# Feed-forward of a gated block: x and z turned by transposing DMAs, two PSUM banks at a time, normalisation on ScalarE, weights laid out ahead

## The chip, the cores and the metric

One core of a Trainium2 chip runs the whole program. The metric is the device time of one execution in microseconds (us); the median of three runs stands for a kernel. A core has five engines that run side by side and meet only at semaphores: TensorE (PE in the rows), VectorE (DVE), ScalarE (ACT), GpSimd (POOL) and SyncE (SP), which here only issues DMAs. Each engine works through its own instructions in order; an instruction that waits holds up everything behind it on its engine.

## The reference

2048 tokens of width 512 (x is 4 x 512 x 512). First an expert layer: each token goes to one of four experts, chosen by its id; expert e has one 512 x 512 matrix, used three times (ctx_2048 is passed as gate, up and down weight). Then a feed-forward layer with quantised operands.

```
x = x + tanh(g_xattn) * experts(layernorm(x), token_ids, ctx, ctx, ctx)
x = x + tanh(g_ffn)   * ffn(layernorm(x), gate_w, gate_b, val_w, val_b, out_w, out_b)

experts: e = min(id // 6250, 3);  y = (silu(h @ W[e].T) * (h @ W[e].T)) @ W[e].T
bit_linear(x, w, b):                      # D = 512, H = 2048
    scale_x = 127 / max(abs(x), per token)
    xq = round(x * scale_x) / scale_x     # clipped to -128..127
    wq = clip(round(w / mean(abs(w))), -1, 1) * mean(abs(w))
    return xq @ wq.T + b
ffn(x) = bit_linear(silu(bit_linear(x, gate)) * bit_linear(x, val), out)
```

## The kernel before

**Routing.** The token ids are sorted by expert into 19 units (`UNITS`) of 128 rows, none with rows of two experts. POOL gathers the rows of a unit from memory by an indirect DMA (`gather`) and, when the unit is finished, scatters the rows with their mean, 1/deviation and token number to a buffer in memory, `x1_rows`, by another (`scatter`).

**Expert units.** Weights and activations are split into a high and a low float16 part, so that a product is 12 matmuls of 512 columns (`product`, line 494). ctx arrives with the wrong axis on the partitions, so TensorE turns it in 16 groups (`ctx_group`, 458); ScalarE makes `w_hi` from PSUM and VectorE `w_lo` (883), four of them POOL. `slot(j)` of TensorE (523) is: turn gu of unit j-1, the first product of unit j, turn h of unit j+1, the second product of unit j-1. VectorE's loop over j (976) makes the normalised rows (`norm`), the low parts (`h_low`, `gu_low`), the product gu, the new rows x1 and their statistics. POOL's loop (361) makes 1/deviation of unit j+2 (`unit_rstd`), that of the finished rows (`x1_rstd`), scatters unit j-2, gathers unit j+4, and rounds two pairs of weight groups (`round_pair`, 341) in twelve consecutive passes, from j = 7 (`W_SLOT` = 8). ScalarE sums their absolute values (`sum_abs`) in units 0 to 11 and takes the sign (`sign_pair`) after the rounding. The three weight matrices are 24 pairs of 128 x 512 groups (`PAIRS`); after the sign TensorE turns each pair in eight transposes (`turn_pair`, 513) and VectorE copies it back (`keep_pair`, 933).

**Hand-over.** SP waits until units 0 to 15 are scattered, then loads the first two tiles of the feed-forward stage (`EARLY`, 256); POOL scatters unit 16 only after these loads have landed (309 to 312). After unit 18 it loads the others.

**Feed-forward stage.** 16 tiles of 128 tokens. Per tile TensorE does 32 matmuls for gate and value (`gate_val`, 579: four chunks c of 512 columns, four matmuls each for gate and value), 16 for the output (`down`, 598), 4 transposes of the quantised x (`turn_x`) and 16 of the quantised z (`turn_z`). The work on a tile is spread over three slots: gate and value of tile t, the quantising of z of tile t-1, and the output of tile t-2. For each chunk VectorE scales PSUM and adds the bias (`pre_gate`, `pre_val`), ScalarE does silu, POOL multiplies the two (`z_chunk`, 385) and VectorE takes the largest absolute value (`z_max`, 1053). From the four maxima come the scales (`z_max_all`, `z_gamma`, `z_scales`); ScalarE rounds z by adding a large number in two halves (`z_round`, 763), POOL subtracts it again (`unshift_z`, 377), TensorE turns each half into PSUM, and ScalarE copies it to SBUF (`z_keep`, 778). x goes the same way: VectorE normalises (`tile_norm`, 1012), ScalarE rounds and subtracts, TensorE turns, ScalarE copies. POOL adds the output bias to the rows and stores by an indirect DMA.

The order on every engine is written out by hand in the functions `ffn_slot` (TensorE 610, ScalarE 782, VectorE 1112) and `slot` (POOL 405); the middle tiles run in a loop with registers.

## Time and profile before

| | |
|---|---|
| median of three runs | 369.0 us (368.78 to 369.78) |
| the profiled execution | 367.59 us, its span 365.5 us |
| mean granted TensorE clock | 0.984 of full speed |
| start until the first product | 0 to 24.1 us |
| expert units | 24.1 to about 164.9 us |
| feed-forward stage | 164.9 us to the end |
| TensorE busy | 90% of the span |
| VectorE, GpSimd, ScalarE busy | 81%, 71%, 63% |

The span runs from the first to the last instruction that the profile records; 2.1 us of the profiled execution lie around it. Busy shares are averages over three stages with different limits, so a term of the change has to be read in its own stage. In a row of the timeline the first number is the start and the second the length, both in us; the brackets tell how long the engine had stood idle and what ended that.

### The profile page before, as it was taken

To read this page: it belongs to the slowest core of one execution; us is meant where nothing else is said; L and a number is where in the kernel's file an instruction comes from. 1 tells how busy PE (TensorE), PEld (TensorE's weight loads), DVE (VectorE), ACT (ScalarE), POOL (GpSimd) and SP (SyncE) were. 2 spreads that over 40 slices of the span, in tenths; PEclk is the share of its full clock that TensorE was granted. 3 is DMA by queue.
4 is the path that set the end of the run, shared out by engine and by line. 5 is a ranking of instruction groups with operands and counts; after the bars stand their busy time and mean duration, and the time that the engine had idled before them with its cause. 6 is when DMAs were issued, how large, how long until landed. Compare 5 with 4: busy or idle time off the path is not lost.

```text
span 365.5 us, 7169 instructions
## 1 busy us (share of the span) xinstructions
PE 328.6 (90%) x1976; PEld 177.8 (49%) x1992; DVE 294.5 (81%) x644; ACT 229.5 (63%) x327; POOL 259.4 (71%) x306
## 2 busy tenths in 40 slices
PE   2858899989998999789779999999999999999972
PEld 2734455546565555454335455544555455554440
DVE  5874777767787866788999899998999889998760
ACT  2837474657874456474467776687766877668650
POOL 2470366568878887847887888888888888888711
PEclk9979999999999999999999999999999999999997
DMA  6969257569312227231101101111011110110011
GB/s 244 302 225 388 57 208 266 179 203 248 126 58 65 84 84 275 70 89 34 32 2 29 59 31 58 58 30 58 29 58 55 31 58 29 59 47 11 29 39 49
DMA packets 24598, 37.03 MB, mean 101 GB/s; under 512 B 4543, under 2 KB 12735, under 8 KB 24320
## 3 DMA queue, kind: packets, MB, share of 16 engines
q1 hardware_dynamic: 20256, 23.38, 20.4%
q0 software_dynamic: 4320, 13.40, 10.6%
q8 instruction: 9, 0.15, 0.2%
q14 instruction: 13, 0.11, 0.1%
HBM read 28.35 MB, written 9.20 MB: 103 GB/s over the span
## 4 chain that ended last, share of the span: by engine, by line
PE 51%; POOL 17%; issue 10%; DVE 10%; DMA 6%; ACT 4%; POOLq 1%; SPq 0%; ACTq 0%; DVEq 0%
PE bank L587 25%; PE bank L605 15%; POOL raw L349 6%; PE bank L503 4%; PE bank L595 4%; POOL x_sb L331 3%; ACT tern L705 2%; POOL xg L302 2%; DMA x_rows<-x_sb,scatter_at 2%; POOL rstd L331 2%; DMA raw<-in_ctx 2%; POOL x_rows L315 1%; PE bank L469 1%; POOL var_eps L328 1%; POOL raw L388 1%
## 5 line engine op out<-in xcount | busy, mean ns | idle before, releaser
L587 PE MATMUL bank<-tern,raw 128*128 128x512 bf16 x512 | 118.2, 379 | 1.0 <-DVE raw L1042 0.7
L388 POOL TENSOR_TENSOR raw<-raw 128x512 f32<-128x512 f32 x63 | 80.3, 1278 | 21.5 <-ACT raw L776 18.1
L503 PE MATMUL bank<-w_hi,turned 128*128 x304 | 73.8, 386 | 9.1 <-DVE turned L915 7.9
L587 PEld LDWEIGHTS bank<-tern,raw 128*128 (+1 forms) x512 | 48.7, 98 | 55.3 <-ACT raw L761 1.3
L776 ACT ACTIVATE raw<-raw 128x512 f32<-128x512 f32 x64 | 39.9, 624 | 47.8 <-DVE raw L1042 46.3
L605 PE MATMUL bank<-tern,raw 128*128 128x512 bf16 x241 | 57.1, 379 | 3.7 <-ACT raw L780 1.9
L1042 DVE SCALAR_TENSOR_TENSOR raw<-bank,raw 128x512 f32<-128x512 f32 x64 | 47.6, 744 | 6.1 <-PE bank L587 5.4
L1050 DVE SCALAR_TENSOR_TENSOR raw<-bank,raw 128x512 f32<-128x512 f32 x64 | 47.6, 744 | 3.0 <-POOL raw L388 0.9
L503 PEld LDWEIGHTS bank<-w_hi,turned 128*128 128x128 f16 x304 | 29.8, 98 | 38.9 <-issue 13.8
L768 ACT ACTIVATE raw<-raw,magic 128x1024 f32 (+1 forms) x32 | 39.2, 1235 | 6.7 <-DVE raw L1069 6.7
L713 ACT ACTIVATE sign_sb<-raw,magic 128x1024 bf16<-128x1024 f32 (+1 forms) x24 | 27.2, 1148 | 25.9 <-POOL raw L349 25.7
L1055 DVE TENSOR_REDUCE raw<-raw 128x1 f32<-128x512 f32 (+1 forms) x64 | 43.1, 674 | 0.0
L503 PE MATMUL bank<-w_lo,turned 128*128 x152 | 39.9, 385 | 0.0
L382 POOL TENSOR_SCALAR raw<-raw,magic,one 128x1024 bf16<-128x1024 f32 x29 | 36.9, 1272 | 3.8 <-ACT raw L768 3.6
L605 PEld LDWEIGHTS bank<-tern,raw 128*128 128x128 bf16 x256 | 24.2, 98 | 29.4 <-ACT raw L780 2.3
L315 POOL DMA_INDIRECT x_rows<-x_sb,scatter_at x19 | 20.5, 1078 | 19.1 <-POOL x_sb L339 15.4
L780 ACT ACTIVATE raw<-bank 128x1024 bf16<-128x1024 bf16 x31 | 31.1, 1006 | 1.0 <-PE bank L595 1.0
L302 POOL DMA_INDIRECT xg<-in_x,gather_at x19 | 18.9, 994 | 16.1 <-DVE gather_at L875 9.3
L349 POOL TENSOR_SCALAR raw<-raw,inv_gam,magic 128x1024 f32<-128x1024 f32 x24 | 28.4, 1191 | 0.6
L893 DVE TENSOR_SCALAR h_sb<-xg,mean_var,rstd 128x512 f32<-128x512 f32 x19 | 11.2, 589 | 20.9 <-POOL rstd L331 19.0
L401 POOL DMA_INDIRECT out<-raw x16 | 16.6, 1038 | 13.9 <-DVE raw L1078 11.6
L705 ACT ACTIVATE tern<-raw 128x1024 bf16<-128x1024 f32 x24 | 25.3, 1053 | 1.1
(115 smaller groups left out, 477.4 us busy)
## 6 DMA issues: line engine op xcount, KB each, us to landing
raw<-x_rows SPq DMA_DIRECT2D x16, 257.5 KB, 2.6
raw<-in_ctx SPq DMA_DIRECT2D x4, 1024.0 KB, 8.2
raw<-in_L_ffn_gate_w SPq DMA_DIRECT2D x4, 1024.0 KB, 9.8
raw<-in_L_ffn_val_w SPq DMA_DIRECT2D x4, 1024.0 KB, 5.1
raw<-in_L_ffn_out_w SPq DMA_DIRECT2D x16, 256.0 KB
raw<-in_L_ffn_gate_b SPq DMA_DIRECT2D x1, 1024.0 KB
raw<-in_L_ffn_val_b SPq DMA_DIRECT2D x1, 1024.0 KB
xg<-in_x,gather_at POOLq DMA_INDIRECT x19, 3.8
```

Of the source, the lines that this page charges most:

```text
L349: nc.gpsimd.tensor_scalar(w, w, inv_gam[:, m:m + 1], magic[:, 0:1], ALU.mult, ALU.add).then_inc(rounded, 1)
L382: nc.gpsimd.tensor_scalar(zi[:, a:b], zq[:, a:b], magic[:, 1:2], one[:, 0:1], ALU.add, ALU.mult).then_inc(zi_made[half], 1)
L388: nc.gpsimd.tensor_tensor(flat(z[:, bass.ds(t % 2, 1), c * D:(c + 1) * D]), s_post[:, c % 2, :], v_pre[:, c % 2, :], ALU.mult).then_inc(z_ ...
L503: last = nc.tensor.matmul(acc[:, :], a[:, k * P:(k + 1) * P], flat(w[:, bass.ds(e4 + k, 1), :]), start=(k == 0 and i == 0), stop=(k == KD ...
L587: last = nc.tensor.matmul(ps[c % 2][:, :].rearrange("p (a b) -> p a b", b=P), flat(xiT[:, bass.ds(t % 2, 1), k * P:(k + 1) * P]), rhs, sta ...
L605: last = nc.tensor.matmul(o_ps[:, :], ziT[:, k, :], tern[:, 2 * G + k, :], start=(k == 0), stop=(k == G - 1))
L705: nc.scalar.activation(flat(tern[:, 2 * p:2 * p + 2, :]), flat(raw[:, 2 * p:2 * p + 2, :]), ACT.Abs, accum_out=abs_sum[:, p:p + 1]).then_i ...
L768: nc.scalar.activation(zq[:, a:b], flat(z[:, bass.ds(t % 2, 1), a:b]), ACT.Identity, scale=flat(sc[:, bass.ds(t, 1), 12:13]), bias=magic[: ...
L776: nc.scalar.activation(s_post[:, c % 2, :], g_pre[:, c % 2, :], ACT.Silu).then_inc(s_made, 1)
L1042: v.scalar_tensor_tensor(g_pre[:, c % 2, :], g_ps[c % 2][:, :], col(t, 3), bias_g[:, c * D:(c + 1) * D], ALU.mult, ALU.add).then_inc(g_mad ...
L1050: v.scalar_tensor_tensor(v_pre[:, c % 2, :], v_ps[c % 2][:, :], col(t, 4), bias_v[:, c * D:(c + 1) * D], ALU.mult, ALU.add).then_inc(v_mad ...
L1055: v.tensor_reduce(col(t, 5 + c), flat(z[:, bass.ds(t % 2, 1), c * D:(c + 1) * D]), AX.X, ALU.max, apply_absolute_value=True).then_inc(zmax ...
```

## The change

**Layout of the weights.** The host now hands over ctx and the three weight matrices with the contracted axis on the partitions, 128 rows of contiguous data each. `ctx_group`, `turn_pair` and `keep_pair` are gone. `w_hi` and `w_lo` are made from SBUF in 8 pairs of 1024 columns instead of 16 groups of 512, all low parts by VectorE. `sign_pair` writes the finished pair. Rounding starts two units earlier (`W_SLOT` = 6). Three tiles are loaded early instead of two, each with its token column.

**Feed-forward stage.** z and x are turned by `dma_start_transpose` from SBUF to SBUF, issued by SP: two of 128 x 1024 for z and one of 128 x 512 for x per tile. `z_keep` and `x_keep` are gone. Gate and value are worked on in two pairs of 1024 columns, each two PSUM banks, instead of four chunks. Gate has two pairs of banks, value one. The second half of `unshift_z` moves from POOL to ScalarE. `tile_norm` moves from VectorE to ScalarE, as a multiplication by 1/deviation and an addition of a shift that VectorE makes (`tile_shift`), two tiles ahead. All loops but TensorE's are written out.

```diff
@@ POOL
+            def z_pair(t, c, width=2 * D):
+                pool.wait_ge(s_made, 2 * t + c + 1)
+                pool.wait_ge(v_made, 2 * t + c + 1)
+                nc.gpsimd.tensor_tensor(z[:, t % 2, 2 * D * c:2 * D * c + width], g_sb[:, c, 0:width],
+                                        v_sb[:, c, 0:width], ALU.mult).then_inc(z_made, 1)
...
+            for t in range(TILES):
+                if t >= 1:
+                    z_pair(t - 1, 1)
+                if t >= 3:
+                    store(t - 3)
+                if 1 <= t < TILES - 1:
+                    add_bias(t + 1)
+                if t >= 1:
+                    unshift_z(t - 1)
+                z_pair(t, 0)
@@ VectorE
+                    for p in range(6, E * KD // 2):
+                        w_low(p)
...
+            for t in range(TILES):
+                if t + 2 < TILES:
+                    tile_shift(t + 2)
+                pre_gate(t, 0)
+                if t >= 1:
+                    z_max(t - 1, 1)
+                    z_max_both(t - 1)
                     z_gamma(t - 1)
                     z_scales(t - 1)
+                pre_val(t, 0)
+                if t + 2 < TILES:
+                    x_max(t + 2)
+                    x_gamma(t + 2)
+                pre_gate(t, 1)
+                if t + 2 < TILES:
+                    x_scales(t + 2)
                 z_max(t, 0)
+                pre_val(t, 1)
+                if 2 <= t < TILES - 1:
+                    finish(t - 2)
@@ ScalarE
+            def ffn_slot(t, before=True, start=False, after=True):
+                if after:
+                    tile_norm(t + 2)
+                silu_gate(t, 0)
+                if before:
+                    z_round(t - 1, 0, start)
+                    z_round(t - 1, 1, start)
+                    unshift_z(t - 1, start)
+                silu_gate(t, 1)
+                if after:
+                    x_round(t + 2)
+                    x_unshift(t + 2)
@@ TensorE
+                pe.wait_ge(x_turned, 16 * (t + 1))
+                gate(t, 0, start)
+                val(t, 0, start)
+                if downs:
+                    down(t - 2, 0, start_down)
+                gate(t, 1, start)
+                val(t, 1)
+                if downs:
+                    down(t - 2, 1)
@@ SP
+            def turn_z(t, half):
+                sp.wait_ge(zi_made[half], t + 1)
+                if t >= 1:
+                    sp.wait_ge(z_read[half], t)
+                sp.dma_start_transpose(ziT[:, half * G // 2:(half + 1) * G // 2, :],
+                                       zi[:, half * H // 2:(half + 1) * H // 2]).then_inc(z_turned[half], 16)
...
+            for t in range(TILES + 1):
+                if 3 <= t < TILES - 1:
+                    load_tokens(t + 1)
+                if t >= 1:
+                    turn_z(t - 1, 0)
+                    turn_z(t - 1, 1)
+                if t + 2 < TILES:
+                    turn_x(t + 2)
+                if t + XT < TILES:
+                    load_rows(t + XT)
```

On POOL in the feed-forward stage, one tile (tile 3) of the kernel before; L388 is `z_chunk`, L395 the output bias, L382 `unshift_z`, L401 the store:

```order
L388 TENSOR_TENSOR raw<-raw 128x512 [waits v_made,s_made]
L395 TENSOR_TENSOR raw<-raw 128x512 [waits xn_made]
L388 TENSOR_TENSOR raw<-raw 128x512 [waits v_made,s_made]
L388 TENSOR_TENSOR raw<-raw 128x512 [waits s_made,v_made,ziT_done1,ziT_done0]
L382 TENSOR_SCALAR raw<-raw,magic,one 128x1024 [waits zq_made0,consts32]
L388 TENSOR_TENSOR raw<-raw 128x512 [waits v_made,s_made]
L382 TENSOR_SCALAR raw<-raw,magic,one 128x1024 [waits zq_made1,consts32]
L401 DMA out<-raw 2048x512 [waits o_made,consts32]
```

The same place of the changed kernel, where L387 is `z_pair`, L400 the store, L394 the bias and L381 `unshift_z`:

```order
L387 TENSOR_TENSOR w_both<-raw 128x1024 [waits v_made,s_made] x2
L400 DMA out<-raw 2048x512 [waits o_made]
L394 TENSOR_TENSOR raw<-raw 128x512 [waits xn_made]
L381 TENSOR_SCALAR w_both<-w_both,magic,one 128x1024 [waits z_turned0,zq_made0]
L387 TENSOR_TENSOR w_both<-raw 128x1024 [waits v_made,s_made] x2
```

Before, `unshift_z` of the former tile stood behind three of this tile's four multiplications; now it stands ahead of both.

On VectorE in the feed-forward stage of the changed kernel, from `pre_gate(t, 0)` (L922) on; L935 is `z_max`, L941 to L950 the scales of z, L930 `pre_val`, L902 to L912 the scales of x:

```order
L922 SCALAR_TENSOR_TENSOR raw<-banks,raw 128x1024 [waits z_made,g_done,xs2_made]
L935 TENSOR_REDUCE raw<-w_both 128x1 [waits z_made]
L941 TENSOR_SCALAR raw<-raw 128x1 [waits zmax_made]
L945 TENSOR_SCALAR raw<-raw 128x1 [waits z_step]
L949 RECIPROCAL raw<-raw 128x1 [waits z_step]
L950 TENSOR_TENSOR raw<-raw,out_gam 128x1
L930 SCALAR_TENSOR_TENSOR raw<-banks,raw 128x1024 [waits z_made,v_done]
L902 TENSOR_REDUCE raw<-raw 128x1 [waits xn_made]
L906 TENSOR_SCALAR raw<-raw 128x1 [waits x_step]
L922 SCALAR_TENSOR_TENSOR raw<-banks,raw 128x1024 [waits z_made,g_done]
L910 RECIPROCAL raw<-raw 128x1 [waits x_step]
```

Before, the same engine took these steps in chunks of 512, with four maxima per tile. Now `pre_val(t, 0)` stands behind the scales of the former tile, and three rows further on, after the two other scales of x, comes the maximum of the pair whose value part it made.

On VectorE at the start of the changed kernel, around unit 0 (L775 is `w_low`, L796 `h_low(1)`, L805 `gu_low(0)`):

```order
L796 SCALAR_TENSOR_TENSOR turned<-banks,turned 128x512 [waits hThi_made]
L783 TENSOR_SCALAR h_sb<-xg,mean_var,rstd 128x512 [waits rstd_made]
L835 TENSOR_TENSOR sign_sb<-sign_sb,banks 128x4
L837 TENSOR_SCALAR sign_sb<-sign_sb 128x19 [waits route_step]
L837 TENSOR_SCALAR sign_sb<-sign_sb 128x19 x2
L838 TENSOR_SCALAR sign_sb<-banks 128x19
L839 TENSOR_TENSOR sign_sb<-sign_sb 128x19 [waits route_step]
L775 SCALAR_TENSOR_TENSOR w_both<-raw,w_both 128x1024 [waits whi_made,route_step]
L775 SCALAR_TENSOR_TENSOR w_both<-raw,w_both 128x1024 [waits whi_made]
```

The two L775 rows are new here; `gu_low(0)` comes behind them.

## Rows read from the trace of the kernel before

**Rows 1.** The page: busy times of the engines, and the chain's shares by engine

```profile
PE 328.6 (90%) x1976; PEld 177.8 (49%) x1992; DVE 294.5 (81%) x644; ACT 229.5 (63%) x327; POOL 259.4 (71%) x306
...
PE 51%; POOL 17%; issue 10%; DVE 10%; DMA 6%; ACT 4%; POOLq 1%; SPq 0%; ACTq 0%; DVEq 0%
```

**Rows 2.** One steady tile: length, then busy PE, PEld, DVE, ACT, POOL, clock

```profile
212.86:224.34 11.48, 11.43 (x68) 5.79 (x69) 10.52 (x24) 8.39 (x11) 9.70 (x9) 1.00 0.16 47
```

**Rows 3.** That tile by line: count, busy us, mean ns of one, idle before

```profile
L587 PE MATMUL bank<-tern,raw 128*128 128x512 bf16 x32 | 7.4, 379 | 0.0
L388 POOL TENSOR_TENSOR raw<-raw 128x512 f32<-128x512 f32 x4 | 5.1, 1279 | 1.3 <-ACT raw L776 1.2
L605 PE MATMUL bank<-tern,raw 128*128 128x512 bf16 x16 | 3.9, 379 | 0.1
L1042 DVE SCALAR_TENSOR_TENSOR raw<-bank,raw 128x512 f32<-128x512 f32 x5 | 3.7, 742 | 0.1
...
L1055 DVE TENSOR_REDUCE raw<-raw 128x512 f32 x4 | 2.7, 674 | 0.0
L382 POOL TENSOR_SCALAR raw<-raw,magic,one 128x1024 bf16<-128x1024 f32 x2 | 2.6, 1282 | 0.3 <-ACT raw L768 0.3
...
L768 ACT ACTIVATE raw<-raw,magic 128x1024 f32 x2 | 2.5, 1236 | 0.3 <-DVE raw L1069 0.3
...
L595 PE MATMUL bank<-ident,raw 128*128 128x128 bf16 x16 | 1.2, 219 | 0.0
...
L576 PE MATMUL bank<-ident,raw 128*128 128x128 bf16 x4 | 0.4, 219 | 0.0
```

**Rows 4.** Timeline of the hand-over: x1 behind the bias loads, scatter, first loads, first gate

```profile
147.44 0.75 DVE L921 SCALAR_TENSOR_TENSOR x_sb<-bank,y_scale,xg 128x512 f32<-128x512 f32 x1 [2.71 <-DMA x_rows<-x_sb,scatter_at]
...
151.48 1.07 POOL L315 DMA_INDIRECT x_rows<-x_sb,scatter_at  x1 [0.81 <-POOL x_sb L339]
...
154.64 0.33 SPq L249 DMA_DIRECT2D raw<-x_rows  x1
...
164.87 5.35 PE L587 MATMUL bank<-tern,raw 128*128 128x512 bf16 x24 [0.22 <-ACT raw L761]
```

**Rows 5.** Timeline of POOL: gather of unit 9, first rounding, second

```profile
67.33 0.98 POOL L302 DMA_INDIRECT xg<-in_x,gather_at  x1 [0.30 <-issue]
...
81.44 2.37 POOL L349 TENSOR_SCALAR raw<-raw,inv_gam,magic 128x1024 f32<-128x1024 f32 x2
...
89.05 2.38 POOL L349 TENSOR_SCALAR raw<-raw,inv_gam,magic 128x1024 f32<-128x1024 f32 x2
```

**Rows 6.** All lines by form: POOL's two-input operation on one column

```profile
L328 POOL TENSOR_TENSOR var_eps<-mean_var,halves 128x1 f32<-128x1 f32 x19 | 3.5, 184 | 19.6 <-DVE mean_var L902 19.5
```

**Rows 7.** Timeline of the end: scales of the last z, its rounding, the last `finish`

```profile
348.81 0.69 DVE L1055 TENSOR_REDUCE raw<-raw 128x1 f32<-128x512 f32 x1
...
349.91 0.17 DVE L1069 RECIPROCAL raw<-raw 128x1 f32<-128x1 f32 x1
...
350.11 2.37 ACT L768 ACTIVATE raw<-raw,magic 128x1024 f32<-128x1024 f32 x2 [2.21 <-DVE raw L1069]
...
358.28 0.75 DVE L1078 SCALAR_TENSOR_TENSOR raw<-bank,raw 128x512 f32<-128x512 f32 x1 [4.41 <-PE bank L605]
```

**Rows 8.** Issues by line: KB of one, median us from issue to landing

```profile
raw<-x_rows SPq DMA_DIRECT2D x16, 257.5 KB, 2.6
...
raw<-in_L_ffn_gate_w SPq DMA_DIRECT2D x4, 1024.0 KB, 9.8
```

**Rows 9.** Timeline of VectorE: `norm` of units 0 and 1, `gu_low(0)`; TensorE: first product

```profile
19.67 1.38 DVE L893 TENSOR_SCALAR h_sb<-xg,mean_var,rstd 128x512 f32<-128x512 f32 x1 [1.97 <-issue]
...
26.53 0.55 DVE L893 TENSOR_SCALAR h_sb<-xg,mean_var,rstd 128x512 f32<-128x512 f32 x1 [1.10 <-POOL rstd L331]
...
33.38 0.69 DVE L915 SCALAR_TENSOR_TENSOR turned<-bank,turned 128x512 f16<-128x512 f32 x1 [0.49 <-ACT turned L696]
...
24.14 3.59 PE L503 MATMUL bank<-w_hi,turned 128*128 x8 [0.78 <-ACT w_hi L679]
```

**Rows 10.** Timeline of VectorE: the reciprocal of tile 0's z

```profile
183.40 0.15 DVE L1069 RECIPROCAL raw<-raw 128x1 f32<-128x1 f32 x1
```

719 lines of the change are left out of this document (250 added, 469 removed).

## The prediction

> **What bounds the kernel now.** I read the page first. TensorE is busy for 90% of the span and makes half of the chain that ended last; GpSimd makes another 17% of it [rows 1]. These are averages, so I cut the time into three stages. The last of them, the feed-forward stage, repeats one tile of 11.48 us, in which TensorE is busy for 11.43 us and all other engines less [rows 2]. There TensorE sets the pace. By line [rows 3], such a tile has 48 matmuls of 512 columns and 20 transposes. 24 such matmuls in a row take 5.35 us, of which the last one's latency is some 0.16, so one is 0.216 us [rows 4] and 48 are 10.4 us. The transposes are the other 1.1 us, and they are what the change takes off TensorE. In the expert units with rounding GpSimd sets the pace: its roundings follow each other every 7.61 us [rows 5]. The start is bound by a chain of small steps.
>
> **The feed-forward tile after the change.** With 48 matmuls TensorE needs 10.4 us. The question is whether another engine, or a circle of waits, needs more. Added up, no engine does: GpSimd has two multiplications of 1024, one rounding step, a bias and a store, 8.4 us; VectorE some 9.5, ScalarE some 8. But the orders of the four engines close a circle. From the scales of tile t-1: ScalarE rounds its first half; GpSimd subtracts (`unshift_z`), which now stands ahead of both multiplications of tile t; GpSimd multiplies pair 0; VectorE takes its maximum, and only then does `pre_val(t, 1)`; GpSimd multiplies pair 1; VectorE takes that maximum and makes the scales of tile t. Each step waits for the one before, by data or by its engine's order, so the sum is a period that no slack elsewhere shortens. Its terms:
> - ScalarE rounding, 1024 columns: 1.24, and GpSimd subtracting: 1.28 [rows 3].
> - Twice the multiplication of 1024. The trace has 512 columns at 1.279 [rows 3] and one column at 0.184 [rows 6], so a column costs 2.14 ns and 1024 cost 2.38. Doubling the instruction gives the upper bound, 2.56. Twice 2.38 is 4.76.
> - Twice the maximum: 0.674 for 512 [rows 3]; with 0.17 for one column [rows 7] as the fixed part that is 1.18, and doubled 1.35. Twice 1.18 is 2.36.
> - `pre_val`: 0.742 for 512 [rows 3], by the same way 1.31, doubled 1.48.
> - The three small steps from the end of the last maximum until ScalarE starts: 350.11 - 349.50 = 0.61 [rows 7].
> - Four other changes of engine. GpSimd stood idle 0.3 us ahead of two roundings [rows 3], 0.15 each; I take 0.1, so 0.4.
>
> The sum is 1.24 + 1.28 + 4.76 + 2.36 + 1.31 + 0.61 + 0.4 = 11.96 us. With the shorter GpSimd rounding of [rows 5] (2.37 / 2 = 1.19) and hops and overlaps cut to the least it is 11.5; with all doubled it is 13.0. I take 11.96, since both ends of the multiplication's line are in the trace. So taking 1.1 us off TensorE buys nothing here: 0.5 us per tile is lost.
>
> The Trainium skill, page GPSIMD Engine Reference, section 3.1, gives 4497 ns for a two-input operation of 2048 float32. By that 1024 would take 2.25 us and the circle 11.7, a forecast 4 us lower. No run here shows that width yet.
>
> **The transposes themselves.** Half of z is 256 KB from SBUF to SBUF. The trace has no such transfer. The nearest row in size is the load of 257.5 KB, which lands 2.6 us after its issue, and the longest landing of this queue is 9.8 us for 1 MB [rows 8]. I take 3. On SP `turn_z` waits for the reads of the tile before, and behind it stand `turn_x`, the row loads and the token loads; GpSimd's `unshift_z` waits for the transfer of a whole tile earlier. With 3 us each has 4 us or more to spare, so the price in a steady tile is nothing. The cover goes when two and a half such transfers fill the period: 11.96 / 2.5 = 4.8 us each. ScalarE's copies from PSUM (1.0 and 0.6 us) leave, a rounding step and `tile_norm` come; it has no part in the circle but `z_round`.
>
> **Start.** GpSimd no longer makes low parts during `norm(0)`, which falls from 1.38 to the 0.55 that `norm(1)` takes [rows 9], and no ctx groups stand between h and the first product. The product starts 1.9 us earlier than 24.14 [rows 9]. But VectorE makes two low parts of 1024 (1.2 each) ahead of `gu_low(0)` at 33.38 [rows 9]. That takes 2.4 us back for the second product. Some is caught up in unit 1, where TensorE had waited: net -0.8, between -2 and +1.
>
> **Expert units.** TensorE loses 192 transposes and VectorE 24 copies of 0.7, all in passes that GpSimd's 7.61 us bound; that is worth nothing. The rounding moves two passes forward. It could first stand at 67.33 + 1.03 = 68.4; two periods of 7.61 later is 83.6, where now it is 81.44 [rows 5]: +2.1. At the other end nothing comes back, since the scatter that SP waits for stands ahead of the last rounding now. The bias loads, which made VectorE wait 2.7 us [rows 4] where GpSimd did not yet need the result, fall two passes earlier, into a pass where it does: +1.0, between 0 and 1.9. SP's first load, at 154.64 [rows 4], comes at 154.6 - 0.8 + 2.1 + 1.0 = 156.9; call it L.
>
> **Hand-over.** The third tile with its tokens puts two more DMAs (0.45 each) ahead of the scatter of unit 16. Then GpSimd scatters 16, 17 and 18 until L + 14.0, adds two biases (2.2), multiplies (2.4), and through maximum, `pre_val`, second multiplication, maximum and scales (0.1 + 1.2 + 1.2 + 0.1 + 2.4 + 0.1 + 1.2 + 0.6) the first scales of z stand at L + 25.5. Before it was 183.55 - 154.64 = 28.9 [rows 4, 10]: 3.4 gained. The first gate product hangs on SP's transpose of x and starts some 10 us after L as before (164.87); it has 1.5 us of slack to the multiplication.
>
> **End.** 15 periods of 11.96, less 1.0 since GpSimd multiplies only 512 columns of the last pair. Before, the last scales stand at 350.08, `finish` starts 8.2 later and the span ends 7.2 after that [rows 7]. Now: VectorE is free 2.3 after the scales, subtracts twice (0.7), the second transpose lands 4.3 later behind the first, 8 matmuls (1.7): 9.3, and 7.2. That is 16.5; each microsecond of a transfer adds one.
>
> **The sum.** 156.9 + 25.5 + 179.4 - 1.0 + 16.5 = 377.3 us of span. The profiled execution has 2.1 more than its span and lies 1.4 under the median: 380.8 us.
>
> **The rivals.**
> - *TensorE's pace holds.* If a multiplication of 1024 cost 1.7 instead of 2.4, or the waits overlapped more than rows show, the period is 10.4 and the time 380.8 - 15 x 1.56 = 357.4. For it: every engine's own sum is under 10.4. Against: the price per column lies between two rows, and the circle is in the order itself. The point where it turns faster is a period of 11.2. With half-way periods 355 to 366. Chance 0.20.
> - *The transposes bound.* Over 4.8 us each they, and not the circle, set the tile. At 5.5 a tile is 13.8 and the time 408; at the 9.8 of the longest landing [rows 8] 24.5 and 569. For it: nothing in the trace shows such a transfer. Against: the same bytes as plain rows land in 2.6. Chance 0.10. The Trainium skill, VectorE: DVE Perf Modes, section The three transpose paths, gives 1309 ns for one square of 128 by DMA; eight in a row would be 10.5 us and the tile 26 us. No run here shows it.
> - *No difference.* The circle at its least (11.5: -6.9) and neither the earlier rounding (-2.1) nor the bias loads (-1.0) felt: 370.8, with a shorter transfer at the end 369. Chance 0.07.
> - *The forecast*, 370 to 390: 0.63.
>
> **How the numbers follow.** I forecast the likeliest, 380.8. The range 364 to 394 takes in the bounds of the period but its doubled end, the no-change case, and the near edges of the two others; about 2 in 10 stay out. A measurement here can tell about 0.3% (1 us) from no change. Faster by more has 0.20, within it 0.06, slower 0.74.
>
> **What would show it.** Right: a steady tile of 11.5 to 12.5 us with TensorE busy about 10.4 of it; the chain of waits going round GpSimd's multiplication, VectorE and ScalarE; 1024 columns on GpSimd at 2.3 to 2.5. Roundings every 7.6 us from about 68. TensorE waiting for VectorE's read of PSUM or for nothing at all, tile by tile, would decide between circle and rival one. A tile bound by SP, or z's transfers over 4.8 us, would show the second. I am wrong at the root if GpSimd's multiplication takes under 1.8.

## The result: 29 us slower, more than twice the forecast loss

| | before | after |
|---|---|---|
| median | 368.89 us (367.34 to 369.78) | 397.75 us (395.18 to 398.16) |
| ratio | | 1.077, 95% interval 1.071 to 1.083 |
| profiled execution, its span | 367.59, 365.5 us | 398.16, 396.4 us |
| steady feed-forward tile | 11.48 us | 12.81 us |

The prediction was 380.8 us, range 364 to 394. The sign was right, and so was the circle of waits through the engines, but the loss is 29 us where 12 were forecast, and the time lies above the range.

The page of the changed kernel, busy times and the chain's shares by engine, as in [rows 1]:

```profile
PE 304.7 (77%) x1399; PEld 141.7 (36%) x1416; DVE 284.0 (72%) x518; ACT 216.2 (55%) x267; POOL 235.6 (59%) x257
...
DVE 29%; PE 28%; POOL 24%; issue 12%; DMA 4%; ACT 1%; POOLq 1%; SPq 0%; DVEq 0%; ACTq 0%
```

TensorE has fallen from 90% to 77%. It made half of the chain before; now VectorE, TensorE and GpSimd share it. That is the picture of a circle through several engines. A steady tile, the columns as in [rows 2]:

```profile
249.90:262.70 12.80, 10.64 (x48) 4.53 (x48) 11.28 (x17) 7.76 (x8) 8.20 (x5) 1.00 0.42 94
```

TensorE is busy for 10.6 us of it, as the 48 matmuls ask, and waits for 2.2. The steps of the forecast circle, in the page's groups (busy time, mean ns of one, idle time before):

```profile
L387 POOL TENSOR_TENSOR w_both<-raw 128x1024 f32<-128x1024 f32 (+1 forms) x32 | 74.8, 2339 | 41.4 <-DVE raw L930 41.4
...
L935 DVE TENSOR_REDUCE raw<-w_both 128x1 f32<-128x1024 f32 x32 | 38.8, 1214 | 28.2 <-POOL w_both L387 28.2
L675 ACT ACTIVATE w_both<-w_both,magic,raw 128x1024 f32<-128x1024 f32 x32 | 38.0, 1233 | 21.6 <-DVE raw L949 21.6
...
L930 DVE SCALAR_TENSOR_TENSOR raw<-banks,raw 128x1024 f32<-128x1024 f32 x32 | 40.8, 1276 | 0.4 <-PE banks L524 0.4
...
L381 POOL TENSOR_SCALAR w_both<-w_both,magic,one 128x1024 bf16<-128x1024 f32 x15 | 17.9, 1193 | 28.4 <-ACT w_both L675 28.4
```

Each duration is within 0.1 us of its term: multiplication 2.34 (forecast 2.38), maximum 1.21 (1.18), rounding 1.23 (1.24), `pre_val` 1.28 (1.31), subtraction 1.19 (1.28). The idle times name the circle: GpSimd's multiplications waited 41.4 us for `pre_val` (L930), VectorE's maxima 28.2 us for the multiplications. And yet a tile is 12.81 us, not 11.96. What is in it that the sum has not? The timeline of VectorE and GpSimd through such a tile (L930 `pre_val(t, 1)`, L960 `finish`, L896 `tile_shift` of the tile after next, L922 `pre_gate(t+1, 0)`, L935 `z_max(t, 1)`, L949 the scales; L387 on POOL the multiplication of pair 1):

```profile
256.13 1.27 DVE L930 SCALAR_TENSOR_TENSOR raw<-banks,raw 128x1024 f32<-128x1024 f32 x1
257.32 0.74 DVE L960 SCALAR_TENSOR_TENSOR raw<-banks,raw 128x512 f32<-128x512 f32 x1
...
257.55 2.35 POOL L387 TENSOR_TENSOR w_both<-raw 128x1024 f32<-128x1024 f32 x1 [2.59 <-DVE raw L930]
...
257.98 1.93 DVE L896 SCALAR_TENSOR_TENSOR raw<-raw 128x1 f32<-128x1 f32 x1
259.84 1.27 DVE L922 SCALAR_TENSOR_TENSOR raw<-banks,raw 128x1024 f32<-128x1024 f32 x1
261.03 1.20 DVE L935 TENSOR_REDUCE raw<-w_both 128x1 f32<-128x1024 f32 x1
...
262.71 0.16 DVE L949 RECIPROCAL raw<-raw 128x1 f32<-128x1 f32 x1
```

`tile_shift` multiplies one column. It takes 1.93 us here and ends at 259.91, just as the multiplication does at 259.90. Behind it stands `pre_gate`, and only then the maximum, which could have started at 260.0 and starts at 261.03. In the first tiles the same instruction took 0.13 to 0.16 us; from 206.73 on it takes 1.93 or 1.94 in each of eleven tiles. It comes to stand beside the multiplication where `finish`, which the first two slots don't have, runs ahead of it. The changed kernel holds a first witness itself: from scales to scales it takes 12.80 to 12.82 us eleven times, once for each of these eleven rows, and 11.73 or 11.74 in three other periods. This is the theory that the experiments test: **an operation with two tensor inputs in SBUF stands still while GpSimd works on SBUF, and holds all that is behind it.** The rivals are that it waits for the loaded rows, or that the pace is set by something else, such as the transposes or the clock.

### The profile page after: what moved, and what is told of

Read it like the earlier page. It is cut to its first block, busy times and chain, and to the rows that moved or that the text cites. A ratio compares the mean times of both kernels' runs of the same rounds, so it can differ in the third digit from the quotient of the medians.

```text
span 396.4 us, 5102 instructions
## 1 busy us (share of the span) xinstructions
PE 304.7 (77%) x1399; PEld 141.7 (36%) x1416; DVE 284.0 (72%) x518; ACT 216.2 (55%) x267; POOL 235.6 (59%) x257
## 3 DMA queue, kind: packets, MB, share of 16 engines
HBM read 28.35 MB, written 9.20 MB: 95 GB/s over the span
## 4 chain that ended last, share of the span: by engine, by line
DVE 29%; PE 28%; POOL 24%; issue 12%; DMA 4%; ACT 1%; POOLq 1%; SPq 0%; DVEq 0%; ACTq 0%
PE banks L524 8%; PE banks L536 8%; POOL raw L356 7%; DVE raw L930 7%; PE banks L514 6%; DVE raw L896 5%; PE banks L461 5%; POOL xg L309 4%; DVE raw L935 4%; DVE raw L922 3%; POOL w_both L387 3%; POOL x_sb L338 3%; DMA x_rows<-x_sb,scatter_at 2%; POOL rstd L338 2%; POOL x_rows L322 2%
## 5 line engine op out<-in xcount | busy, mean ns | idle before, releaser
L461 PE MATMUL banks<-w_both,turned 128*128 x456 | 109.6, 392 | 23.1 <-DVE turned L805 21.2
L387 POOL TENSOR_TENSOR w_both<-raw 128x1024 f32<-128x1024 f32 (+1 forms) x32 | 74.8, 2339 | 41.4 <-DVE raw L930 41.4
L524 PE MATMUL banks<-tern,raw 128*128 128x512 bf16 x243 | 62.9, 394 | 34.3 <-DVE raw L930 33.5
L461 PEld LDWEIGHTS banks<-w_both,turned 128*128 128x128 f16 x456 | 45.7, 100 | 74.3 <-issue 32.5
L536 PE MATMUL banks<-tern,w_both 128*128 128x512 bf16 x255 | 63.6, 396 | 8.0 <-DMA w_both<-w_both 7.9
L514 PE MATMUL banks<-tern,raw 128*128 128x512 bf16 x254 | 60.2, 379 | 0.1
L935 DVE TENSOR_REDUCE raw<-w_both 128x1 f32<-128x1024 f32 x32 | 38.8, 1214 | 28.2 <-POOL w_both L387 28.2
L675 ACT ACTIVATE w_both<-w_both,magic,raw 128x1024 f32<-128x1024 f32 x32 | 38.0, 1233 | 21.6 <-DVE raw L949 21.6
L524 PEld LDWEIGHTS banks<-tern,raw 128*128 (+1 forms) x256 | 23.3, 100 | 72.4 <-DVE raw L930 47.4
L687 ACT ACTIVATE raw<-raw 128x1024 f32<-128x1024 f32 x32 | 33.6, 1050 | 16.3 <-DVE raw L922 16.3
L922 DVE SCALAR_TENSOR_TENSOR raw<-banks,raw 128x1024 f32<-128x1024 f32 x32 | 40.9, 1278 | 0.7 <-PE banks L514 0.7
L930 DVE SCALAR_TENSOR_TENSOR raw<-banks,raw 128x1024 f32<-128x1024 f32 x32 | 40.8, 1276 | 0.4 <-PE banks L524 0.4
L514 PEld LDWEIGHTS banks<-tern,raw 128*128 (+1 forms) x256 | 25.1, 98 | 30.4 <-issue 0.5
L381 POOL TENSOR_SCALAR w_both<-w_both,magic,one 128x1024 bf16<-128x1024 f32 x15 | 17.9, 1193 | 28.4 <-ACT w_both L675 28.4
L783 DVE TENSOR_SCALAR h_sb<-xg,mean_var,rstd 128x512 f32<-128x512 f32 x19 | 10.4, 546 | 29.8 <-POOL rstd L338 29.8
L400 POOL DMA_INDIRECT out<-raw x16 | 16.8, 1049 | 18.1 <-DVE raw L960 15.9
```

What stands on the lines that cost most here:

```text
L387: nc.gpsimd.tensor_tensor(z[:, t % 2, 2 * D * c:2 * D * c + width], g_sb[:, c, 0:width], v_sb[:, c, 0:width], ALU.mult).then_inc(z_made, 1)
L461: last = nc.tensor.matmul(acc[:, :], a[:, k * P:(k + 1) * P], flat(w[:, bass.ds(e4 + k, 1), :]), start=(k == 0 and i == 0), stop=(k == KD ...
L514: last = nc.tensor.matmul(g_ps[c][:, b, :], flat(xiT[:, bass.ds(t % 2, 1), k, :]), tern[:, k * HC + 2 * c + b, :], start=(k == 0), stop=(k ...
L524: last = nc.tensor.matmul(v_ps[:, b, :], flat(xiT[:, bass.ds(t % 2, 1), k, :]), tern[:, G + k * HC + 2 * c + b, :], start=(k == 0), stop=( ...
L536: last = nc.tensor.matmul(o_ps, ziT[:, k, :], tern[:, 2 * G + k, :], start=(k == 0), stop=(k == G - 1))
L675: nc.scalar.activation(zq[:, a:b], flat(z[:, bass.ds(t % 2, 1), a:b]), ACT.Identity, scale=flat(sc[:, bass.ds(t, 1), 12:13]), bias=magic[: ...
```

## Where the rest went

The span is 19.1 us longer than forecast: the first scales of z come 4.7 later (start and expert units 1.8, hand-over 2.9), the 15 periods take 187.4 us and not 178.4 (9.0), the end 22.0 and not 16.5 (5.5). In the 9.0 the held `tile_shift` is 11.8, and the rest of the circle is 2.8 shorter than forecast. The time is over its forecast by 17.0 only, since the sum had added 3.5 us from the span to the median, and it was 1.4. Start and expert units, timelines of POOL, VectorE and TensorE (first gather, `norm(0)`, first product, first rounding), as in [rows 5, 9]:

```profile
12.16 3.25 POOL L309 DMA_INDIRECT xg<-in_x,gather_at  x1 [8.96 <-DVE gather_at L765]
...
21.62 0.55 DVE L783 TENSOR_SCALAR h_sb<-xg,mean_var,rstd 128x512 f32<-128x512 f32 x1 [1.74 <-POOL rstd L338]
...
24.85 5.30 PE L461 MATMUL banks<-w_both,turned 128*128 x12 [1.50 <-DVE turned L796]
...
69.96 2.37 POOL L356 TENSOR_SCALAR raw<-raw,inv_gam,magic 128x1024 f32<-128x1024 f32 x2
```

`norm(0)` is as short as forecast, 0.55, but it comes 2 us later than before, because the first gather took 3.25 us to issue where the next took 0.97. VectorE made two low parts (two inputs in SBUF, 2.34 us from 12.03) meanwhile. The first product takes 5.30 us. That is no loss of the change: the row of 3.59 us in [rows 9] holds only the eight matmuls on `w_hi`, and the four on `w_lo` follow it in the kernel before:

```profile
27.52 1.88 PE L503 MATMUL bank<-w_lo,turned 128*128 x4
```

From 24.14 to 29.40 that product took 5.26 us, at a granted clock of 0.50 from 24 to 28 us. The slow clock of the start was there before.

The hand-over, timelines of SP, TensorE, POOL and VectorE (first row load, product of unit 18, first multiplication, first scales), as in [rows 4, 10]:

```profile
158.71 0.33 SPq L237 DMA_DIRECT2D raw<-x_rows  x1
...
165.65 5.20 PE L461 MATMUL banks<-w_both,turned 128*128 x12 [6.31 <-DVE turned L805]
...
177.86 2.36 POOL L387 TENSOR_TENSOR w_both<-raw 128x1024 f32<-128x1024 f32 x1
...
186.90 0.16 DVE L949 RECIPROCAL raw<-raw 128x1 f32<-128x1 f32 x1
```

The last product of the expert stage follows 6.3 us in which TensorE was idle, and takes 5.20 us instead of the usual 2.76. The scatter of unit 18 and the first multiplication come behind it. From the multiplication on the hand-over goes as forecast (9.2 us to the scales, forecast 9.3), so all of its 2.9 us are lost ahead of it.

The end, VectorE and TensorE, as in [rows 7], and the windows around it (length, busy PE, PEld, DVE, ACT, POOL, granted clock, share and GB/s of the DMA engines):

```profile
374.26 0.16 DVE L949 RECIPROCAL raw<-raw 128x1 f32<-128x1 f32 x1
...
377.37 1.29 DVE L1019 TENSOR_SCALAR w_both<-w_both 128x1024 bf16<-128x1024 f32 x2
...
383.14 6.54 PE L536 MATMUL banks<-tern,w_both 128*128 128x512 bf16 x16 [6.48 <-DMA w_both<-w_both]
...
389.72 0.75 DVE L960 SCALAR_TENSOR_TENSOR raw<-banks,raw 128x512 f32<-128x512 f32 x1 [11.07 <-PE banks L536]
```

```profile
378.00:382.00 4.00, 0.00 (x0) 0.00 (x0) 0.65 (x2) 0.00 (x0) 0.88 (x1) 0.60 0.72 143
382.00:386.00 4.00, 2.86 (x7) 1.04 (x8) 0.00 (x0) 0.00 (x0) 0.00 (x0) 0.50 0.34 54
```

TensorE idles for 6.5 us; the granted clock falls to 0.50, which is the lower of its two levels, 1.2 GHz, and the last 16 matmuls take 6.54 us, where 16 took 3.66 one tile earlier.

## The experiments

All start from the changed kernel. Times are medians; the ratios are to the kernel before (368.4 to 368.9 us on the same chips).

### One tensor input instead of two

```diff
-                v.scalar_tensor_tensor(col(t, 7), of[:, MEAN:MEAN + 1], -1.0, of[:, RSTD:RSTD + 1],
-                                       ALU.mult, ALU.mult).then_inc(shift_made, 1)
+                v.tensor_scalar(col(t, 7), of[:, MEAN:MEAN + 1], of[:, RSTD:RSTD + 1], -1.0,
+                                ALU.mult, ALU.mult).then_inc(shift_made, 1)
```

> One edit to the changed kernel: tile_shift (line 896, one column) reads 1/deviation as a scalar operand instead of as a second tensor, in the same place. Theory A (an operation with two tensor inputs in SBUF stands still while GpSimd multiplies, and holds pre_gate and z_max of the next step): the row falls from 1.93 us to 0.2, z_max(t,1) follows the end of GpSimd's multiplication by 0.1 instead of 1.13, and the late period falls from 12.81 to about 11.8; the time from 397.7 to 384 to 386. Rival B (the row is long because it waits for the loaded rows, or for anything but its own operands): the row stays 1.9 and the time 397 to 398. Rival C (any VectorE operation on those columns stands still beside GpSimd): the same as B. Rival D (the row does get short, but the pace is set by something else, such as the transposing DMAs or the clock): row 0.2, period still 12.5 to 12.8, time over 394.

386.48 us (385.75 to 387.06), ratio 1.050 (1.046 to 1.054): 11.3 us gained by one operand. Timeline of POOL and VectorE through a tile:

```profile
242.16 2.36 POOL L387 TENSOR_TENSOR w_both<-raw 128x1024 f32<-128x1024 f32 x1 [2.59 <-DVE raw L930]
...
242.60 0.20 DVE L896 TENSOR_SCALAR raw<-raw 128x1 f32<-128x1 f32 x1
242.72 1.27 DVE L922 SCALAR_TENSOR_TENSOR raw<-banks,raw 128x1024 f32<-128x1024 f32 x1
244.56 1.22 DVE L935 TENSOR_REDUCE raw<-w_both 128x1 f32<-128x1024 f32 x1 [0.57 <-POOL w_both L387]
...
245.76 1.27 POOL L394 TENSOR_TENSOR raw<-raw 128x512 f32<-128x512 f32 x1
...
246.25 0.17 DVE L949 RECIPROCAL raw<-raw 128x1 f32<-128x1 f32 x1
246.33 0.73 DVE L950 TENSOR_TENSOR raw<-raw,out_gam 128x1 f32<-128x1 f32 x1
```

The row is 0.20, beside the same multiplication; the maximum waits for GpSimd and for nothing else; the scales follow each other every 11.74 us. Theory A holds for this instruction, and rivals B, C and D fall. VectorE's L922 ran beside the multiplication for 1.27 us, not slower than alone: it has one input in PSUM and one in SBUF. And a second witness has appeared in the last row. L950, one column, two inputs in SBUF, took 0.14 in 15 of the 16 tiles of the changed kernel. Here it meets GpSimd's bias addition (245.76 to 247.03), takes 0.73 and ends at 247.06.

The Trainium skill, page SBUF — State Buffer, section Who interferes with whom, says that a VectorE instruction with two SBUF inputs contends with a GpSimd instruction that reads SBUF, and that the loser is blocked until the other's end, not slowed. The trace of the changed kernel agrees: 1.93 us for one column, ending with the multiplication.

The number of tensor inputs is not the whole rule, though. `norm(0)` of the kernel before is a TENSOR_SCALAR like the row of e1, with one tensor and two scalar operands, on 512 columns. It took 1.38 us from 19.67, where `norm(1)` took 0.55 [rows 9], and this is what GpSimd did meanwhile:

```profile
19.62 3.56 POOL L359 TENSOR_TENSOR w_lo<-tern,w_hi 128x512 f16<-128x512 f32 x3
```

No run here takes apart why that one was long and the one-column form of e1 never is.

### The same instruction elsewhere

```diff
+            tile_shift(2)
             for t in range(TILES):
-                if t + 2 < TILES:
-                    tile_shift(t + 2)
                 pre_gate(t, 0)
...
                 pre_val(t, 0)
+                if t + 3 < TILES:
+                    tile_shift(t + 3)
```

> One edit to the changed kernel: tile_shift with its two tensor inputs unchanged, but one tile further ahead and behind pre_val(t,0), where GpSimd does not multiply (it subtracts or is idle). Theory A: 0.15 to 0.3 us beside an idle GpSimd, at most 1.2 if the subtraction holds it as well; period 11.8 to 12.2, time 384 to 391. Rival B or C (the row is slow wherever it stands): 1.9 us there too; it then stands in the circle itself, so the time stays at 397 or rises. Rival D: row short, time over 394.

388.32 us (386.41 to 389.92), ratio 1.056 (1.051 to 1.060), 9.4 us gained; period 11.74. The instruction now mostly meets GpSimd's subtraction:

```profile
249.84 1.19 POOL L381 TENSOR_SCALAR w_both<-w_both,magic,one 128x1024 bf16<-128x1024 f32 x1 [0.77 <-ACT w_both L675]
...
250.22 0.82 DVE L896 SCALAR_TENSOR_TENSOR raw<-raw 128x1 f32<-128x1 f32 x1
```

It is held there too, until 251.04 (the subtraction ends at 251.03), though that GpSimd operation has only one tensor input. But nothing of the circle waits for what stands behind it, and the period is that of e1. A stall costs what is queued behind it, not its own length. In slot 0 the moved instruction asks for the rows of tile 3 before they are there. It waits 3.81 us for their DMA with all of VectorE's work behind it, and the first scales stand at 189.58 instead of 187.54 in e1. That is the likely source of the 1.8 us between the two medians, though in the two profiled executions the end gives it back: both spans are 384.7.

### The circle cut

The edit of e1, and:

```diff
                 if t + 2 < TILES:
                     x_scales(t + 2)
+                pre_val(t, 1)
                 z_max(t, 0)
-                pre_val(t, 1)
```

> The edit of e1, and on VectorE pre_val(t,1) ahead of z_max(t,0) instead of behind it. My prediction's circle (period = ScalarE rounding + GpSimd subtraction + two multiplications with a maximum and pre_val between them + maximum + scales) loses 1.2 + 1.3 us by it, 9.3 us are left, and TensorE with 48 matmuls at 0.216 should set the pace: period 10.4 to 10.7, TensorE busy all of it, time 366 to 371. If the transposing DMAs are not hidden (the rival of the prediction): TensorE waits for them, period 11 or more, time over 374. If the circle is not what sets the pace: the time of e1, 384 to 386.

360.98 us (360.85 to 361.38), ratio 0.981 (0.977 to 0.984): 1.9% faster than the kernel before, and 36.8 us faster than the changed one, by one operand and two exchanged lines. The period is 10.36 us, with TensorE busy for all of it:

```profile
235.10:245.46 10.36, 10.36 (x50) 4.69 (x48) 9.72 (x17) 7.76 (x8) 8.20 (x5) 1.00 0.55 116
```

So the circle was the bound, with 1.2 + 1.3 us of it in that order of two lines, and without it TensorE's 48 matmuls are. Each transposing DMA is hidden.

> Only the reordering of e3; tile_shift keeps its two tensor inputs and its place. By theory A the maximum and finish (1.2 + 0.7 us) now lie between the start of GpSimd's multiplication of pair 1 and tile_shift, so it is held for 0.4 to 0.6 us only, behind which pre_gate still comes in time: period 10.4 to 10.9, time 367 to 374. If the stall costs the same wherever the order puts it: about 1 us per tile more than e3, 381 to 385.

The exchange of the two lines alone, with `tile_shift` as it was, gives 365.01 us (363.4 to 367.89), ratio 0.992 (0.989 to 0.995), a little under what I expected and 4.0 over e3. The steady period is 10.36 as well. VectorE's rows, and POOL's two multiplications and bias addition, which the first of them meets:

```profile
178.56 4.67 POOL L387 TENSOR_TENSOR w_both<-raw 128x1024 f32<-128x1024 f32 x2
183.19 1.08 POOL L394 TENSOR_TENSOR raw<-raw 128x512 f32<-128x512 f32 x1
...
182.09 2.21 DVE L896 SCALAR_TENSOR_TENSOR raw<-raw 128x1 f32<-128x1 f32 x1
...
194.41 1.47 DVE L896 SCALAR_TENSOR_TENSOR raw<-raw 128x1 f32<-128x1 f32 x1
...
246.66 0.67 DVE L896 SCALAR_TENSOR_TENSOR raw<-raw 128x1 f32<-128x1 f32 x1
```

0.67 us in the steady tiles is covered, as expected. In the first two slots `finish` is absent, and there it is held for 2.21 (until 184.30, past the multiplications and to the end of the bias addition at 184.27) and for 1.47 on the path: the first scales come at 187.09 instead of 184.99, the second at 198.67 instead of 194.22. The price of the same stall is 0 or some 2 us, by what stands behind it.

### What the transposes cost

On e3, behind each half of z in the queue of SP, in tiles 1 to 8:

```diff
+                if 1 <= t < 9:
+                    spare = raw_flat[:, 2 * G * D + (2 * t - 2 + half) * D:2 * G * D + (2 * t - 1 + half) * D].bitcast(bf16)
+                    sp.dma_start_transpose(spare.rearrange("p (h m) -> p h m", m=P),
+                                           flat(tern[:, 2 * half:2 * half + 2, :])).then_inc(spare_turned, 16)
```

> On e3, two more transposing DMAs of 128 x 1024 per tile in tiles 1 to 8, from the weights to free memory, behind each half of z in SP's queue; nothing reads them. They nearly double the traffic of the transposes. My prediction (not felt in a steady tile until two and a half transfers fill the period): with 1.2 us of issue and about 1.7 us of DMA time each, the queue is at some 85%; x and the second half land 1.3 to 3 us later, which the orders cover: period 10.36 in tiles 1 to 8 as in 9 to 14, time 361 to 362. Rival (the transposes are close to the bound): the period of the doubled tiles is 11 to 14, time 366 to 390.

361.19 us (360.45 to 361.26), ratio 0.979 (0.976 to 0.982), as e3. The scales follow each other at 10.36 with twice the transposes of z as without. The DMA view of 200 to 262 us, share of the queue, and then medians to landing:

```profile
q1 hardware_dynamic: 30649, 8.75, 74.4%
...
raw<-tern SPq DMA_TRANSPOSE x13, 3.2
w_both<-w_both SPq DMA_TRANSPOSE x12, 3.2
...
raw<-raw SPq DMA_TRANSPOSE x6, 3.8
```

The queue's share is 74.4% where e3 has 46.0%. Only x's transposes land later, 3.8 instead of 2.5 us. The second rival of the prediction is refuted with room to spare.

### The clock behind idle time

On e3, extra matmuls into a free bank (`keep_clock(n, acc)` issues n of 512 columns):

```diff
+            pe.wait_ge(whi_made, 1)
+            keep_clock(32, bank[4])
             turn_h(0)
...
+            keep_clock(27, bank[4])
             e4 = expert_of(UNITS - 1)
             pe.wait_ge(guTlo_made, UNITS)
...
             for t in range(TILES - 3, TILES):
+                if t == TILES - 1:
+                    for _ in range(26):
+                        nc.tensor.matmul(bank[3], tern[:, 0, 0:P], tern[:, 0, :], start=True, stop=True)
                 down(t, 0)
```

> On e3. Extra matmuls without a use, into a free bank, where TensorE stood idle longest: 32 ahead of turn_h(0), 27 ahead of the product of unit 18, 26 ahead of the last tile's down. Theory (the matmuls behind long idle time are slow because the granted clock has fallen to the half, 1.2 of 2.4 GHz): the 16 last matmuls fall from 6.28 to about 3.6 us, the 12 of unit 18 from 5.10 to about 2.8, the first product from 4.16 to about 2.8, the first transposes of h from 1.12 to 0.6. End -2.7, hand-over -2.3, start up to -1.9 as far as it is felt: 354 to 357. Rival (they are slow because their weights or data arrive late, or because GpSimd and the DMAs hold the path): their length stays, time 361 or later by what the extra matmuls delay. A second rival: the clock rises, but the stages wait for something else just behind (scatter, store), and under 2 us are gained.

357.17 us (356.09 to 358.38), ratio 0.969 (0.965 to 0.973), 3.8 less than e3. TensorE's timeline:

```profile
24.48 5.30 PE L465 MATMUL banks<-w_both,turned 128*128 x12 [1.50 <-DVE turned L806]
...
165.42 2.76 PE L465 MATMUL banks<-w_both,turned 128*128 x12 [0.89 <-DVE turned L815]
...
344.82 3.40 PE L542 MATMUL banks<-tern,w_both 128*128 128x512 bf16 x15 [0.94 <-DMA w_both<-w_both]
```

The product of unit 18 falls from 5.10 (e3) to 2.76, the last matmuls from 6.28 to some 3.6 (one of the 16 is missing in the record). These two were slow by the clock.

What that was worth is read from the traces of e3 and e5. The end, from the last scales on, is 2.6 us shorter. The hand-over, from the row load to the first scales, is 1.8 shorter, but the 15 periods behind it take 1.1 more (the first 10.36 instead of 9.23), which leaves 0.7. Another 1.35 us come ahead of the row load, and most of that is not the edit's. In the pass of the bias loads TensorE idles for some 2.6 us in both, and from 138 to 140 us the granted clock was 0.50 in e3 and 1.00 in e5; from one scatter to the next that pass took 7.48 and 6.27 us. Over the traces it goes together: 7.3 to 7.8 us with a fallen clock in e1, e3, e4, e7 and e8, and 6.27 with a full one in the changed kernel, e2 and e5. What decides it no run tells.

At the start nothing was gained. The transposes of h did fall from 1.12 to 0.66, but the product takes 5.30, with a granted clock of 0.50 from 24 to 30 us, although TensorE had worked on the extra matmuls from 10.9 to 20.6. So my reading for the start, that filling the time ahead of the transposes is enough, failed.

> e10 with extra matmuls at the start without a gap until the first product: 44 ahead of turn_h(0), 6 behind it. If the idle 1.7 and 1.5 us around the transposes were what let the granted clock fall to 0.50 at 24 to 30 us in e5: the first product takes 2.8 instead of 4.2 to 5.3 us and the time falls by 1 to 2.5, 352 to 353.5. Rival (the clock falls by what TensorE did before, not by the gap, or the 44 take longer than the idle time and hold the transposes): the product stays at 4 to 5.3, or starts later, time 354 to 356.

This one stands on e10, below, and fills the gaps around the transposes too, with 44 matmuls ahead of `turn_h(0)` and 6 behind it. The first product takes 2.76 us, at 24.41. Now the second is the slow one, 4.06, behind 2.06 us idle, at a granted clock of 0.63 and 0.51 (30 to 34 us). The first rounding comes 1.3 us earlier than in e10, and yet the time is 360.09 us (358.64 to 361.62), ratio 0.977 (0.973 to 0.981), not below e10. That filling the gap keeps the clock for the first product is supported; that it pays is neither shown nor refuted, since in this run, as in e10, the extra matmuls of the hand-over hold the product of unit 18 (see e10; here by 2.5 us, from 165.7 to 168.26) and hide what was gained ahead of it.

### Smaller terms of the sum

Rounding one unit later, on e3:

```diff
-    W_SLOT = 6
+    W_SLOT = 7
...
-            with act.Fori(PAIRS // 2, W_SLOT + PAIRS // 2) as j:
+            with act.Fori(PAIRS // 2, UNITS - 1) as j:
                 slot(j, pairs=True)
-            slot(UNITS - 1, after=False)
+            slot(UNITS - 1, after=False, pairs=True)
```

> On e3, the rounding of the weights one unit later (W_SLOT 7 for 6). My prediction charged 2.1 us for moving it forward by two units, so one back should give 1.0: first rounding some 6.5 us later instead of 7.5 earlier, SP's first row load (159.12 in e3) at 158.1, time 360.0. Rival (the units in front are bound by something that takes 7.5 anyway, or the signs at the end now hold the tiles' first ScalarE steps): 361 or more.

359.24 us (358.88 to 359.56), ratio 0.974 (0.971 to 0.977), 1.7 less than e3. SP's first row load stands at 157.69 instead of 159.12. By these two traces the price for one unit was 1.4, where the prediction had 1.05. A row load's place is only good to about a microsecond: in the other traces with `W_SLOT` = 6 it stands between 157.77 and 159.96. The times themselves don't overlap.

The low parts behind the statistics, on e3:

```diff
-            for p in range(2):
-                w_low(p)
             unit_stats(0)
-            w_low(2)
+            w_low(0)
             norm(0)
-            w_low(3)
+            w_low(1)
             h_low(0)
             unit_stats(1)
+            w_low(2)
+            norm(1)
+            w_low(3)
             w_low(4)
-            norm(1)
```

> On e3, VectorE makes the first two low parts of the weights (two tensor inputs in SBUF, 1024 columns) behind the statistics of unit 0 instead of ahead of them. Theory (they hold GpSimd, which writes the descriptors of the first gather meanwhile: 3.26 us there, 0.95 to 1.25 for the others): the first gather takes 1.0 to 1.3, unit_stats(0) starts at 15.8 to 16.2 instead of 17.91, norm(0) at 19.5 to 20.0 instead of 21.67; time -1 to -2: 359 to 360. Rival (the first gather is long for its own sake, as the first of its kind): it stays 3.2, nothing is gained, and the low parts come later: 361 to 362.

Both halves of my theory came true in the trace and the time did not move: 360.89 us (360.57 to 361.28), ratio 0.979 (0.976 to 0.982).

```profile
12.16 1.17 POOL L309 DMA_INDIRECT xg<-in_x,gather_at  x1 [8.96 <-DVE gather_at L765]
...
19.52 0.55 DVE L783 TENSOR_SCALAR h_sb<-xg,mean_var,rstd 128x512 f32<-128x512 f32 x1 [1.74 <-POOL rstd L338]
...
31.70 4.45 PE L461 MATMUL banks<-w_both,turned 128*128 x12 [0.22 <-issue]
```

The first gather is 2.1 us shorter than in e3 and `norm(0)` 2.1 us earlier. But the low parts moved behind it now stand ahead of the product gu(0), which starts at 30.08 (29.97 in e3), and TensorE's second product is slow, 4.45 for 2.76, as long as products at the lower clock are. The gain ended one step on.

The Trainium skill, page SBUF — State Buffer, section SBUF: two separate sides, tells of GpSimd unable to write a DMA's descriptors while a VectorE operation in a 2-port mode holds the shared port; in Who interferes with whom it infers that an operation with two SBUF inputs would not do that. Here two such operations go with 3.25 us for one indirect DMA, which ends 1.04 us behind them (15.41 and 14.37), and without them it is 1.17. The measurement decides: these held it.

### Together

The edits of e3 and e6, and those of e5 but for the 32 matmuls at the start:

> e3 with the later rounding of e6 and the extra matmuls of e5 at the hand-over and the end, without those at the start. If the gains add: 361.0 - 1.7 (e6) - 3.8 (e5) = 355.5, ratio to the kernel before 0.965, 354.5 to 357. If they overlap (in e6 TensorE's idle time ahead of unit 18's product was already shorter, 3.9 us, and its matmuls 4.4): 356 to 357.

356.94 us (356.48 to 357.71), ratio 0.969 (0.965 to 0.972): 40.8 us under the changed kernel and 12 under the one before, the lowest median, though not to be told from e5. The gains of e5 and e6 don't add. With the clock kept, rounding one unit later saves nothing that can be told from e5: the row load stands at 158.07 against 157.77 there, the first scales at 181.48 against 181.87.

On this, with `W_SLOT = 8`, the last two roundings move into GpSimd's wait ahead of the scatter of unit 16, and their signs follow on ScalarE:

```diff
                     x1_rstd(j - 2)
+                    if j == UNITS - 1:
+                        round_pair(PAIRS - 2)
+                        round_pair(PAIRS - 1)
                     scatter(j - 2)
...
-                if W_SLOT <= j + 1 < W_SLOT + PAIRS // 2:
+                if W_SLOT <= j + 1 < UNITS:
...
             x_unshift(1)
+            sign_pair(PAIRS - 2)
+            sign_pair(PAIRS - 1)
             ffn_slot(0, before=False)
```

> e9 with the rounding one unit later still (W_SLOT 8), the last two roundings ahead of the scatter of unit 16, where GpSimd waits some 8 us for the row loads, and their two signs on ScalarE behind the x steps of tile 1. Theory (GpSimd's rounding sets the pace of the units it shares, 7.6 against some 6.2): 1.4 us less, 354. Rival (VectorE or ScalarE now sets the pace there, or the signs hold tile 0's silu): 355.5 or more.

359.34 us (358.56 to 363.23), ratio 0.978 (0.974 to 0.983), 2.4 worse than e9. Timelines of VectorE and TensorE (x1 behind the bias loads, the low part of gu of unit 18; the turn of gu, the 27 extra matmuls, the product of unit 18):

```profile
149.43 0.75 DVE L824 SCALAR_TENSOR_TENSOR x_sb<-banks,y_scale,xg 128x512 f32<-128x512 f32 x1 [2.90 <-DMA x_rows<-x_sb,scatter_at]
...
164.44 0.68 DVE L818 SCALAR_TENSOR_TENSOR turned<-banks,turned 128x512 f16<-128x512 f32 x1
...
161.98 5.99 PE L447 MATMUL banks<-w_both 128*128 128x512 f16 x27
167.81 2.75 PE L468 MATMUL banks<-w_both,turned 128*128 x12
```

The rounding itself is not what cost, by this trace: the row load stands 1.1 us earlier than in e9, and the first scales 2.6 later. The loss lies between them, and the extra matmuls make it. The product of unit 18 needs the low part of gu, which is ready at 165.12, and starts only at 167.81, behind the last of the 27. In e9 the low part is ready at 164.91 and the matmuls are over by then: the product starts at 165.10. They began later here, at 161.98 instead of 159.27, because the turn of gu ahead of them did. The likely reason is the bias loads. They hang on the signs of the first 16 pairs, so they move later too, to 140.19 from 133.66 in e9, and the scatter that VectorE's x1 waits for lands later: 2.90 us of waiting, where e9 has 1.07. It is the same wait as in [rows 4], 2.71 there. No run has e10 with fewer extra matmuls, so what its rounding alone is worth stays open. With the 2.6 us taken off, an estimate, it would be some 356.7, as e9, and not the 354 of the theory.

## The prediction, point by point

- **Bound before**: right. TensorE's 10.4 us for 48 matmuls came out as 10.36 in e3.
- **The circle, 11.96 us**: right in kind and in its terms, as e1 shows, where it is alone: 11.74. The 15 periods in e1 take 175.6 us, 2.8 less than forecast. By its number alone the measured 12.81 lies within my bounds on the period, 11.5 to 13.0 (the doubled terms add up to 12.83). That is chance: the upper bound stood for doubled durations, and none was doubled.
- **What failed is the step that is not there.** The prediction gives VectorE's small steps only a place in its total of 9.5 us and never asks which of its instructions meet a GpSimd operation. `tile_shift` stood in no sum. It costs 1.07 us in eleven tiles, 11.8 us, and e1 gave 11.3 back. Without it my forecast of the period would have been 0.2 too high and the whole, as e1's 386.5, inside the range. A warning stood in [rows 9]: `norm(0)` at 1.38 beside GpSimd, `norm(1)` at 0.55, if not of the same form. I used that row as a gain that would come and did not ask where the changed kernel makes such a meeting anew.
- **The order as the cause**: I wrote that `unshift_z` ahead of both multiplications closes the circle. That is one side of it. The cheaper cut was on VectorE, where `pre_val(t, 1)` stands behind `z_max(t, 0)` with no need (e3: 25.5 us less than e1).
- **The transposes, 3 us each and hidden**: right. They land after 3.2 and 2.5 us in e3, and e8 doubles those of z at no price; the price of 10.5 us for eight squares is out. That TensorE's clock falls behind them at the end was not in the term.
- **Start, -0.8**: wrong sign. The first rounding stands at 69.96. The forecast was 68.4 by the order alone, so the start cost +1.6, and the bound to +1 covered part of it. The gain on `norm(0)` was eaten by the gather that the low parts hold; but e7 shows that even without that the next steps take the time back. The first product varies by itself: it took 5.30, 4.16, 4.83 and 5.11 us in otherwise like starts (e9, e3, e6, e8), and the first roundings of e3 (69.06) and e8 (70.03) lie apart by as much as their first products, 1.0.
- **Rounding earlier, +2.1**: right or a little low (1.4 a unit in e6). **Bias loads, +1.0**: right, 0.98 us of waiting at 135.54. The first row load at 158.71 is 1.8 over the forecast 156.9: 2.4 from the start (+1.6 for -0.8), less 0.6 between the first rounding and the row load.
- **Hand-over, 25.5 us**: it took 28.35. The term said that TensorE had slack, and took the product at full clock. Its 12 matmuls cost 2.4 more, and e5 got 2.3 of that back in the row. Up to the first scales, though, e5 is only 1.8 shorter than e3, so about 1 us of the 2.9 has no cause shown.
- **End, 16.5 us**: it took 22.0. Of the 5.5 the clock is about 2.9 (6.54 against 3.63 in e9). I also counted only the 8 matmuls behind the last transfer: the first 8 wait as well, since TensorE could start only 5.1 us after the first subtraction had ended (some 378.0). The two subtractions took 1.29 us together, where 0.7 stood in the sum, and the terms written there add up to 9.0, not 9.3.
- **The rivals**: the first is out for the changed kernel, whose multiplication took 2.34 us and not 1.7. Its period of 10.4 came only with the circle cut by another edit (e3), and the time there is 361, not 357. The others are out. None had a VectorE instruction held by GpSimd, and the range, built from these rivals, ended at 394.

**Left open**: what the clock does at the start. In the changed kernel the granted clock is recorded as 1.00 from 24 to 30 us though 12 matmuls take 5.30; in e5 it is recorded as 0.50 and they take the same. Whether the record or another cause is at work there no run tells. The same gap of 1.50 us stood ahead of first products of 4.16 and of 5.30 us (e3, e9), so the gap alone does not set their length.
